# A decoder layer on one core: ScalarE issues the k stack transfers of the first three tiles, and the orders and PSUM banks are laid out anew

## What is computed

```python
x1 = x + min_gru(rmsnorm(x))                 # sigmoid, tanh, a scan along the rows
x2 = x1 + sliding_attn(rmsnorm(x1))          # 16 heads of 8 columns, causal, softmax
y1 = layernorm(x + x2 + glu_ffn(rmsnorm(x2)))   # 512 hidden columns
y2 = layernorm(y1 + cross_attention(y1, ctx))   # one head of 128
out = layernorm(y2 + mixture(y2))            # 8 experts, the best 2 per row
```

## Time and profile before

| | |
|---|---|
| median of 3 runs | 226.48 us (226.40 to 226.54) |
| profiled execution, its own time | 226.43 us |
| span of that execution, first to last instruction | 224.5 us |
| around the span | 1.93 us |
| busy: TensorE products, TensorE weight loads | 207.8 us, 173.5 us |
| busy: VectorE, ScalarE, GpSimd | 183.7, 172.1, 140.3 us |
| granted TensorE clock, mean | 0.994 |

### The profile page before, as it was taken

How to read it: one execution, slowest core, us unless ns; L and a number is a source line. 1 busy time by engine, 2 the same in 40 slices (tenths; PEclk the granted TensorE clock), 3 DMA queues, 4 the chain that set the end, 5 groups by cost and what they waited for, 6 DMA issues and landing times.

```text
span 224.5 us, 6962 instructions
## 1 busy us (share of the span) xinstructions
PE 207.8 (93%) x2170; PEld 173.5 (77%) x2170; DVE 183.7 (82%) x667; ACT 172.1 (77%) x663; POOL 140.3 (62%) x302
## 2 busy tenths in 40 slices
PE   7889999999999999999999999999989999998840
PEld 3568988999988799799778988798786899884310
DVE  3573775579879789988998999989988897999984
ACT  4799988987798796889699889986668867646730
POOL 5464535637568775777468766975648847547452
PEclk9999999999999999999999999999999999999997
DMA  4988745555742324002400555445460000000001
GB/s 99 252 256 191 181 110 134 149 149 137 172 107 52 105 55 108 0 7 49 108 1 4 123 140 127 109 116 102 127 154 13 5 25 15 16 0 1 12 23 35
DMA packets 33716, 20.05 MB, mean 89 GB/s; under 512 B 20497, under 2 KB 31249, under 8 KB 33681
## 3 DMA queue, kind: packets, MB, share of 16 engines
q1 hardware_dynamic: 32992, 19.35, 34.2%
q10 hardware_dynamic: 688, 0.26, 0.4%
HBM read 14.16 MB, written 5.24 MB: 86 GB/s over the span
## 4 chain that ended last, share of the span: by engine, by line
PE 49%; DVE 14%; DMA 9%; SPq 8%; issue 7%; ACT 7%; POOL 5%; POOLq 0%; DVEq 0%; ACTq 0%
PE ps L966 8%; DMA k_stack<-qk_scratch 5%; PE ps L931 5%; PE ps L843 4%; PE ps L1048 4%; SPq L276 4%; PE ps L898 4%; PE ps L920 4%; PE ps L989 4%; DMA ctx_sb<-in_ctx_dram 3%; PE ps L900 2%; PE ps L877 2%; PE ps L857 2%; DVE acc L2488 2%; ACT probs L1707 2%
## 5 line engine op out<-in xcount | busy, mean ns | idle before, releaser
L2373 DVE TENSOR_REDUCE neg_max<-ps 128x4 f32<-128x512 f32 x64 | 43.1, 677 | 4.7 <-PE ps L900 4.4
L1707 ACT ACTIVATE probs<-ps 128x512 f32<-128x512 f32 x64 | 38.4, 606 | 4.8 <-PE ps L920 4.5
L464 POOL TENSOR_TENSOR lrs<-mv,neghalf 128x1 f32<-128x1 f32 x48 | 26.5, 553 | 24.0 <-DVE mv L2418 8.4
L464 POOL TENSOR_TENSOR rs<-ss,neghalf 128x1 f32<-128x1 f32 x48 | 27.1, 567 | 20.7 <-ACT junk L1626 20.5
L966 PE MATMUL ps<-xT,guT 128*128 128x128 f32 x256 | 34.0, 276 | 0.0
L1048 PE MATMUL ps<-w_moe,y2T 128*128 128x512 f32 x64 | 32.6, 599 | 0.4 <-ACT terms L1786 0.4
L966 PEld LDWEIGHTS ps<-xT,guT 128*128 128x128 f32 x256 | 31.2, 192 | 0.3
L524 POOL TENSOR_SCALAR_AFFINE_SELECT probs<-probs 128x600 f32<-128x600 f32 x32 | 24.2, 758 | 8.1 <-ACT probs L1707 7.8
L898 PE MATMUL ps<-k_stack,q_stack 125*128 125x128 bf16 x256 | 24.9, 219 | 1.3 <-DMA k_stack<-qk_scratch 1.3
L920 PE MATMUL ps<-q_stack,k_stack 128*128 128x128 bf16 x256 | 24.8, 219 | 0.0
L920 PEld LDWEIGHTS ps<-q_stack,k_stack 128*128 128x128 bf16 x256 | 18.8, 99 | 3.8 <-issue 2.3
(11 more groups left out here) (156 smaller groups left out, 584.9 us busy)
## 6 DMA issues: line engine op xcount, KB each, us to landing
q_stack<-qk_scratch SPq DMA_DIRECT2D x48, 96.0 KB
k_stack<-qk_scratch SPq DMA_DIRECT2D x48, 96.0 KB
qk_scratch<-qk_parts SPq DMA_DIRECT2D x16, 192.0 KB, 2.2
ctx_sb<-in_ctx_dram SPq DMA_DIRECT2D x4, 256.0 KB, 3.5
qk_scratch<-qk_parts SPq DMA_DIRECT2D x16, 64.0 KB, 2.4
out_dram<-x_all SPq DMA_DIRECT2D x16, 64.0 KB, 1.6
x_all<-in_x_dram SPq DMA_DIRECT2D x2, 256.0 KB, 3.1
raw<-in_L_ffn_Wi_dram SPq DMA_DIRECT2D x1, 512.0 KB, 6.0
```

What stands on the lines that cost most here:

```text
L464: nc.gpsimd.tensor_tensor(dst, src, neghalf[:], ALU.pow).then_inc(S[rsd], 1)
L1707: nc.scalar.activation(probs[:, b, n, :, :], view("probs", 4 * k + n), ACT.Exp, scale=HD ** -0.5).then_inc(S["att_p"], 1)
L2373: nc.vector.tensor_reduce(neg_max[:, b, QUARTER * n:QUARTER * n + QUARTER], view("scores", 4 * k + n), AX_X, ALU.max, negate=True).then_in ...
```

## The change

The k parts of tiles 0, 1 and 2 are no longer issued in `parts_stack` on SyncE. A new step `k_stacks(k)` in ScalarE's list issues them, after waiting for the same saves. The lists of all five engines and the banks are written anew, and some semaphore waits go or come, since an order makes some of them needless and others needed. The steps themselves are the same, but for two more products of the zero tile on TensorE.

```diff
+K_ON_ACT = (0, 1, 2,)
...
                     sp.dma_start(q_stack[rows, r, :, :], part_rows(scratch[b, PARTS + c:2 * PARTS + c])).then_inc(S["stacked_%d" % r], 16)
-                    sp.dma_start(k_stack[rows, r, :, :], part_rows(scratch[b, 0:PARTS])).then_inc(S["stacked_%d" % r], 16)
+                    if k not in K_ON_ACT:
+                        sp.dma_start(k_stack[rows, r, :, :], part_rows(scratch[b, 0:PARTS])).then_inc(S["stacked_%d" % r], 16)
...
+            def k_stacks(k):
+                b, r = k % 2, k % RING
+                act.wait_ge(S["rows_k_set"], k + 1)
+                act.wait_ge(S["parts_saved_%d" % b], 32 * (k // 2 + 1))
+                for c in range(PARTS):
+                    rows = slice(c * PARTS * HD, (c + 1) * PARTS * HD)
+                    nc.scalar.dma_start(k_stack[rows, r, :, :], part_rows(scratch[b, 0:PARTS])).then_inc(S["stacked_%d" % r], 16)
```

SyncE's list, its later half:

```diff
             parts_save(13)
-            store(3)
             max_stack(11)
             parts_stack(13)
             parts_save(14)
+            store(1)
             max_stack(12)
             parts_stack(14)
-            store(4)
             parts_save(15)
-            store(5)
             max_stack(13)
             parts_stack(15)
+            store(2)
             max_stack(14)
+            store(3)
+            store(4)
             max_stack(15)
+            store(5)
             store(6)
```

```diff
             moe_logits(15)
+            moe_experts(15, 0)
             moe_experts(15, 1)
-            moe_experts(15, 0)
```

More of the change, by code:

```diff
@@ L49 @@
[L49 to L68, removed]
+    "w_gru": "6",
+    "gru_turn": "1174566554546344",
+    "w_qkv": "0",
+    "gru_gates": "1432352436700703",
+    "ctx_turn": "2070711467206215",
+    "gru_turn_back": "0756532312451634",
+    "w_kq": "2",
+    "w_ox": "3",
+    "qkv_turn": "2727276712752702",
@@ new lines @@
+    "ctx_project": "5253022066451625",
+    "qk_project": "0620572531764761",
+    "v_project": "4010702560065000",
+    "w_ei": "3",
+    "w_m0": "7",
+    "w_up": "3",
+    "w_ej": "7",
+    "scores": "1057761236226364401235474651415444631032627167416167367332436606",
+    "w_gate": "6",
+    "w_out": "3",
+    "w_m1": "1",
+    "max_turn": "1463275032024406",
+    "probs": "7403371305550241606204433106643157562136206715516420256431042700",
+    "att_values": "4502771230726442",
+    "att_back": "5215671135211142",
@@ L963, in ffn_hidden @@
                 b = k % 2
+                after(pe, "ffn_xT", k + 1)
                 bank_free(pe, fill, k)
@@ L1084, in _ @@
-            w_ej()
-            gru_gates(4)
+            ctx_turn(2)
+            v_project(0)
+            gru_turn_back(2)
+            w_ei()
+            ctx_project(1)
+            ctx_project(2)
+            qkv_turn(1)
+            ctx_turn(3)
+            gru_gates(3)
+            ctx_project(3)
+            qk_project(1)
+            ctx_turn(4)
+            v_project(1)
+            gru_turn(4)
             ctx_turn(5)
             qkv_turn(2)
-            ctx_project(3)
+            w_m0()
@@ L1163, in _ @@
             scores(3, 2)
+            scores_turned(2, 1)
+            att_back(1)
+            scores(3, 3)
             ffn_gate(0)
-            scores_turned(2, 1)
-            scores(3, 3)
             scores_turned(2, 2)
-            gru_turn_back(7)
             att_turn(1)
@@ L1188, in _ @@
             ctx_project(11)
-            gru_turn_back(8)
+            scores_turned(3, 0)
             xat_turn_probs(0)
@@ L1202, in _ @@
             scores(5, 1)
+            gru_turn_back(8)
+            qkv_turn(7)
             moe_turn(0)
@@ L1827, in _ @@
+            qk_high(1)
+            ctx_copy(4)
+            ctx_copy(5)
+            v_copy(1)
+            qkv_normalize(2)
+            ctx_copy_kv(3)
+            gru_squares(8)
+            qkv_copy(2)
+            k_stacks(0)
+            qk_middle(1)
+            w_m0()
             gru_copy(4)
-            gru_squares(7)
-            ctx_copy(4)
+            ctx_copy_kv(4)
+            ctx_copy(6)
+            ctx_copy_kv(5)
+            gru_normalize(6)
             gru_copy(5)
-            qk_high(1)
@@ L1832, in _ @@
-            qkv_normalize(2)
-            w_ej()
-            qkv_copy(2)
-            qk_middle(1)
-            v_copy(0)
             gru_tanh(4)
             qk_high(2)
-            ctx_copy_kv(3)
+            qkv_squares(3)
+            w_ej()
+            gru_copy(6)
             gru_tanh(5)
-            w_m0()
-            qkv_squares(3)
-            ctx_copy(5)
-            ctx_copy_kv(4)
+            ctx_copy(7)
+            k_stacks(1)
             qk_middle(2)
-            gru_normalize(6)
@@ L1861, in _ @@
             ctx_copy_kv(6)
             qkv_normalize(4)
-            gru_copy(7)
-            ctx_copy(8)
-            ctx_copy_kv(7)
-            qkv_copy(3)
-            qkv_squares(5)
-            qk_high(3)
-            qkv_normalize(5)
-            exponentials(0, 0)
-            qk_middle(3)
-            gru_copy(8)
+            k_stacks(2)
+            qk_middle(3)
+            exponentials(0, 0)
+            gru_copy(8)
+            qkv_squares(5)
+            ctx_copy_kv(7)
             ctx_copy(9)
```

1296 lines of the change are left out of this document (640 added, 656 removed).

## The result

The changed kernel takes **229.88 us** (4 runs, 229.20 to 230.00) against 226.51 (4 runs): ratio 1.0142, 95% interval 1.0122 to 1.0163. The profiled execution took 229.2 us with a span of 227.5. The forecast was 227.0, at most 229.0: the direction was right, the size was not.

What follows compares the result with a forecast made beforehand. The prediction took TensorE to bound the kernel, its products filling 207.8 of 224.5 us. From the profiled 226.43 us, + 0.9 - 0.35 gave 226.98, so 227.0 us for the median, range 225.0 to 229.0.

Steps and rivals of the forecast that it cites:

- The first term, the three k_stacks at +0.9: Nine issues on ScalarE ahead of exponentials(0, 3) make it and att_values(0) late: +0.9 us, between 0 and +3.2.
- TensorE has the same set of steps ahead of att_values(0) as before: Step at the first attention: TensorE has nothing to put into the gap that ScalarE's lateness leaves, +0.9 us.
- the banks at "I take 0": TensorE's bank conflicts in the new order: not visible in another order's trace, taken as 0 and left to the range.
- SyncE's side at 0: Three issues fewer per moved stack on SyncE, 1.2 us less, gain nothing on the path: 0.
- The other moves on SyncE: max_stack(3) goes behind the six issues of stack 5, some 2.4 us: taken as 0, up to +0.5.
- Stores leave the way of the last stacks: Without store(4) ahead of tile 15's save, TensorE's wait at scores(15, 0) goes: -0.35 us, ends 0 and -1.3.
- The last pair of expert products at 0: The last two groups of expert products change places at the kernel's end; their order doesn't reach the end: 0.
- The two products of the zero tile at 0: Two more products on TensorE ahead of gru_turn_back(0), covered by the wait for the scan: 0, uncovered up to 0.4.
- the sign that the prediction went by: gru_turn_back, behind the zero tile's product, still waited 0.17 us for VectorE, so added products would be covered.
- Faster: Rival: issues fall into ScalarE's gaps, exponentials(0, 3) by 36.4 us, stack waits of 1.3 us go: 225.2 us, chance 0.33.
- No change: Rival: TensorE makes up the late start in later stages, where other engines set the pace: 226.5 us, chance 0.22.
- Much slower: Rival: ScalarE comes to k_stacks before the save has landed and waits, +3.2 - 0.35: 229.3 us, chance 0.08.

Runs made afterwards that it cites:

- k_back_on_sp: Changed kernel with its new orders and banks, but SyncE issues the k parts of the first three tiles again: 230.19 us, ratio 1.0165.
- k_on_act_old_orders: Kernel before with its own orders and banks, only the k parts of tiles 0, 1 and 2 moved to ScalarE: 229.02 us, ratio 1.0107.
- new_start_old_rest: Changed kernel's orders and banks with the move up to the first attention, then those of the kernel before: 229.44 us, ratio 1.0136.
- changed_one_transfer: Changed kernel with one transfer a part instead of three, 24 rows outermost: 229.56 us, ratio 1.0154.
- old_start_new_rest: Orders and banks of the kernel before up to the first attention, then the changed kernel's, all k parts on SyncE: 228.92 us, ratio 1.0109.

## Why the prediction was wrong

**The first term, the three k_stacks at +0.9, was mis-sized, and its step was the wrong one.** The step reads "near to the filled end, since the order is written for these issues". In the old orders the nine issues cost 2.85 at exponentials(0, 3) and 2.88 at att_values(0): of the 2.1 us of idle time I counted on, 1.1 took in issues (3.96 - 2.85). The rest of the gaps couldn't be used. I read them as room; a likelier reading, argued and not tested by itself, is that ScalarE there waits for TensorE or GpSimd, which wait for ScalarE's step before, so that the gap moves along with a delay. The price of an issue was right: 1.33 us for three in the changed kernel, 0.44 each.

**The step that failed in the changed kernel is "TensorE has the same set of steps ahead of att_values(0) as before"**, with the banks at "I take 0" and no term for the sequence. I compared sets, which are indeed equal, and the time lies in the sequence, together with its banks. The new orders without the move have the whole lateness (41.05, +2.77, in k_back_on_sp; +2.64 with the move), the first 16 us of them having a share of 0.76 to 0.84 and the rest up to 1.93, the seam included. ScalarE then waits 3.8 us for TensorE, and the issues go into that time and cost nothing. So the +0.9 and the orders' 0 were both wrong, in opposite directions: the issues are covered and the orders cost 2.6. att_values(0) at 40.92 against my 39.2 shows it.

**SyncE's side at 0** isn't contradicted, as far as the intervals tell, but the runs hold both sides of the move, and a small gain there could cancel a small cost on ScalarE: without the move the ratio is 1.0165 (1.0124 to 1.0207), with it 1.0142 (1.0122 to 1.0163). The other moves on SyncE, at 0 too, held: from 42 to 75 us TensorE shows no wait.

**Stores leave the way of the last stacks, -0.35.** The sign I asked for came, scores(15, 0) without a wait (172.88), and TensorE's waits for stacks from 60 to 190 us fell from 1.3 to this row of the waits of the kernel after:

```profile
PE ps L899 <- DMA k_stack<-qk_scratch: 0.4, 1, 0.4
```

The lateness fell by 0.33 up to att_values(15). But k_on_act_old_orders, with the stores where they were, gave back as much: 2.88 at tile 0, 2.51 at tile 15. By tile the two agree: +2.9 at tile 10, +2.47 at tile 12 in each. So the size was right by accident, and the stores aren't shown to be its cause. The 0.35 itself was read too high: the row of scores(15, 0) shows a wait of 0.18.

**The last pair of expert products at 0** held: from the last moe_turn to VectorE's last step it is 8.08 us against 8.12. What I left at 0 in the tail, the other orders, cost 0.61: from att_values(15) to that turn it is 28.93 instead of 28.28. Two products of tile 14 that wait 1.78 for their bank's reader stand right ahead of the turn, and VectorE's y for it is ready at 216.56 + 0.38, 0.51 later than before if one counts from att_values(15); so the two products hold the turn back by no more than 0.13, and the rest is VectorE's, for a reason that stays open. With the old rest, from att_values(15) to the end takes 36.77 us again (new_start_old_rest).

**The two products of the zero tile at 0** held by the sign that the prediction went by: behind the three products that now stand there, the turn still waits 0.55 for VectorE.

```profile
9.48 0.81 PE L781 MATMUL ps<-warm 128*128 128x512 bf16 x3
10.85 0.33 PE L844 MATMUL ps<-ident,gru_h 128*128 128x128 f32 x1 [0.55 <-DVE gru_h L2372]
```

TensorE's busy time grew by 1.2 us, not 0.4; the shown lengths of pipelined products don't say why.

**The rivals.** *Faster* fell at the point it named: exponentials(0, 3) at 39.01, not by 36.4. *No change* needed later stages to make up the delay. They made up 0.33 of 2.64 in 147 us. The Trainium skill (Perfetto Trace Analysis, Identifying the Most-Contended Engine) has TensorE's headroom judged by the share of weight loads among other things, 76% here, rather than by that of products, 92%. The trace doesn't bear out that the remaining quarter was room for this: all of TensorE's shown waits from 60 to 190 us come to 0.4 us, and there was next to nothing to make up from. *Much slower* had nearly the right number, 229.3, by the wrong mechanism: in the changed kernel's trace ScalarE didn't wait for the save, its issues follow the copy ending at 21.79 at once, at 21.77. It was a near thing, since SyncE's issues, which wait for the same save, start at 21.77 too; in new_start_old_rest and changed_one_transfer ScalarE did wait, for 0.8 us.

## What to carry to other kernels

Compare two orders by their sequence around each hand-over, not by the set of steps ahead of a point: here equal sets, with other banks, differed by 2.6 us. An idle gap of a nearly full engine isn't always room. In the old orders three moved issues of 1.3 us cost 0.7 to 1 us where other engines wait for the step right behind them; they cost nothing where ScalarE stood waiting for another engine anyway. So look at what stands behind the place before moving something there. If transfers are too many for one queue, first see whether one pattern can do the work of several; two issues in place of six gave 0.3 to 0.6% in the old orders, where moving them to another engine gave none.

## What was not expected of the hardware

**The outermost dimension of a transfer.** The same bytes to the same stack, with 3 or with 24 rows outermost, gave 297.77 and 225.48 us. The traffic of the first, by queue (packets, MB, share of 16 engines):

```profile
q1 hardware_dynamic: 31936, 19.35, 22.0%
```

TensorE waited 50.9 us for stacks in all, at a DMA share of 22%, so the queue as a whole was far from full. Not all of the 71 us are the transfers' own: TensorE's granted clock fell while it waited so, 0.78 between 25 and 45 us. The Trainium skill (DMA: Bandwidth & Descriptors, Rules for kernel authors) says that a transfer is spread over no more engines than the outermost dimension allows, and gives a leading broadcast of few copies as the example to avoid. By the same page's rule for the number of engines (section Why a DMA increments its semaphore by 16 and not by 1) it would be, as an estimate, 3 engines against 12. The times agree; no view here shows single engines.

**The landing of a save** varies from trace to trace. Its second transfer (64 KB) in the windows around the first save, issue to landing last, took 3.5 us in the kernel after and 2.0 before:

```profile
qk_scratch<-qk_parts SPq DMA_DIRECT2D x1, 64.0 KB, 3.5
```

In old_start_new_rest, whose order up to there is that of the kernel before, it took 3.4. I can't say what sets it; part of the differences between single traces of the start may come from it, where ScalarE or TensorE waits for the save or the stack behind it: the change's own orders up to the first attention gave 40.92 in the changed kernel, 41.05 without the move and 41.67 in new_start_old_rest.
